# The fold and the spread of the step sums move to another engine, and ScalarE scales the transposed sequence tile by the step sizes

## The reference

```python
scale = max(max|w| / 127, 1e-8)                  # per table row
h  = clip(round(w / scale), -127, 127) * scale   # row of the token
x0 = layernorm(h)                                # (h - mean) / sqrt(var + 1e-5)
z, xBC, dt = split(x0 @ in_proj_w.T)
dt = softplus(dt + dt_bias)                      # the step sizes, 6 heads
x, B, C = split(silu(conv4(xBC)))                # 384, 128, 128 channels
A_cum = cumsum(dt * A)
L  = exp(segsum(dt * A))                         # decays, 128 x 128 per head
y  = ((C B^T) * L) @ (x * dt) + D * x            # "x * dt" is what xd holds
h1 = h + gate * rmsnorm(y * silu(z)) @ out_proj_w.T
...                                              # layernorm, two routers, experts
```

## Time and profile before

| what | value |
|---|---|
| median of 3 runs | 1080.34 us (1077.37 to 1080.86) |
| the profiled execution's own time | 1070.86 us |
| its span | 1069.1 us |
| PE busy over the span | 925.8 us (87%) |
| DVE busy | 692.9 us (65%) |
| ACT busy | 583.3 us (55%) |
| POOL busy | 518.9 us (49%) |

### The profile page before, as it was taken

The page is one execution under the profiler, slowest core; times in us unless marked ns, Lnnn a source line. Parts: engine busy times, 40 slices in busy tenths (PEclk is TensorE's granted clock), DMA queues, the critical chain, the costliest instruction groups (busy, mean ns, idle before and its releaser), DMA issues.

```text
span 1069.1 us, 19874 instructions
## 1 busy us (share of the span) xinstructions
PE 925.8 (87%) x5743; PEld 602.2 (56%) x5744; DVE 692.9 (65%) x2047; ACT 583.3 (55%) x1195; POOL 518.9 (49%) x590
## 2 busy tenths in 40 slices
PE   0778898888988998889889788899988999999985
PEld 0233455455544654555445556677766676777774
DVE  3788999999999999999979515576671221212120
ACT  2767886787768767877775343233232323233330
POOL 6232545356354362561522526433427777775552
PEclk9899999999999999999998789999998999999997
DMA  4920011011101110110000122123431212222220
GB/s 101 320 62 5 16 46 43 5 47 46 46 3 45 45 44 5 46 47 31 3 31 30 49 62 79 49 73 110 147 92 48 69 50 66 56 63 77 66 61 18
DMA packets 50001, 61.54 MB, mean 58 GB/s; under 512 B 22524, under 2 KB 41688, under 8 KB 49412
## 3 DMA queue, kind: packets, MB, share of 16 engines
q0 software_dynamic: 16704, 30.54, 10.0%
q1 hardware_dynamic: 28580, 24.93, 7.7%
q10 hardware_dynamic: 4640, 5.13, 1.6%
HBM read 36.24 MB, written 25.92 MB: 58 GB/s over the span
## 4 chain that ended last, share of the span: by engine, by line
PE 43%; DVE 25%; ACT 14%; issue 9%; POOL 6%; DMA 1%; DVEq 0%; ACTq 0%; POOLq 0%
DVE xbc L1429 9%; PE cx L1213 7%; PE yb L1213 7%; PE mm L1201 6%; PE mm L1197 5%; PE sg L1197 4%; POOL list_c L534 4%; PE mm L1051 4%; PE mm L1055 3%; ACT ht L897 2%; DVE mix L1449 2%; ACT h L688 2%; DVE st L1319 2%; DVE ybuf L1462 2%; ACT xbc L716 1%
## 5 line engine op out<-in xcount | busy, mean ns | idle before, releaser
L1429 DVE SCALAR_TENSOR_TENSOR xbc<-mm,cw,xbc 128x508 f32<-128x508 f32 (+2 forms) x231 | 168.5, 741 | 24.1 <-ACT xbc L716 18.2
L1051 PE MATMUL mm<-xt_a,win_a 128*128 128x512 f32 x248 | 145.1, 669 | 37.7 <-DVE xbc L1429 28.8
L897 ACT ACTIVATE ht<-mm,b1s 128x256 f32<-128x256 f32 x102 | 44.7, 472 | 222.2 <-PE sg L1201 219.7
L509 POOL TENSOR_TENSOR ybuf<-ybuf,zs 128x384 f32<-128x384 f32 x64 | 69.5, 1085 | 105.4 <-DVE ybuf L1462 105.3
L586 POOL DMA_INDIRECT xg<-hr_dram,ids x80 | 80.6, 1008 | 80.7 <-DVE res L1756 44.3
L605 POOL DMA_INDIRECT out_dram<-osb,ids_s x80 | 81.9, 1023 | 64.4 <-DVE osb L1766 38.4
L716 ACT ACTIVATE xbc<-mm,cb,cw 128x512 f32<-128x512 f32 x77 | 56.6, 775 | 95.4 <-PE mm L1055 95.4
L1766 DVE TENSOR_TENSOR osb<-cx,res 128x192 f32<-128x192 f32 x40 | 14.2, 356 | 127.3 <-PE cx L1213 125.7
L1197 PE MATMUL mm<-fx_a,w1a_t 128*128 128x256 f32 x240 | 81.9, 424 | 13.7 <-issue 7.6
L1201 PE MATMUL mm<-fx_b,w1b_t 64*128 64x256 f32 x240 | 85.3, 436 | 0.0
L1201 PE MATMUL sg<-fx_b,w1b_t 64*128 64x256 f32 x240 | 85.3, 436 | 0.0
(11 more groups left out here) (271 smaller groups left out, 2056.8 us busy)
## 6 DMA issues: line engine op xcount, KB each, us to landing
hr_dram<-hr SPq DMA_DIRECT2D x16, 768.0 KB
w2s<-in_w2c_dram SPq DMA_DIRECT2D x4, 576.0 KB, 7.8
w2s_u<-in_w2u_dram ACTq DMA_DIRECT2D x4, 576.0 KB
list_c<-fill SPq DMA_DIRECT2D x2, 1032.0 KB, 12.6
list_u<-fill SPq DMA_DIRECT2D x2, 1032.0 KB, 18.9
w1a<-in_w1c_dram SPq DMA_DIRECT2D x4, 384.0 KB, 6.6
w1a_u<-in_w1u_dram ACTq DMA_DIRECT2D x4, 384.0 KB
xg<-hr_dram,ids POOLq DMA_INDIRECT x80, 3.1
```

The source lines that it names most:

```text
L509: nc.gpsimd.tensor_tensor(ybuf[:, p, :, js], ybuf[:, p, :, js], zs[:, p, :, js], ALU.mult).then_inc(s_y2, 1)
L1051: mmul(tile_bank(g2, m)[:, :], win_a[:, column(m):column(m) + P], xt_a[:, p, :], start=True, stop=False)
L1429: ins = stt(out=dst_[:, :, back:L], in0=src[:, :, 0:L - back], scalar=cw[:, m, TAPS - 1 - back:TAPS - back], in1=dst_[:, :, back:L], op0=A ...
```

## The change

- `xd` (L1445, one VectorE instruction for a sequence) is removed from `weights(j)`. A new ScalarE step `steps_in(j)` makes it with six activations of 64 columns, each with a head's step size as its scale. It waits for the `cbm` of the same j (the counter of the chain "ssd") and stands at four places of ScalarE's order: ahead of `decays(0)`, ahead of `squares`, ahead of `start(4)`, and between `decays(3)` and `silus`. TensorE's `y(j)` now waits for both `xd` and `mix`, and `cbx(j)` for both readers of `cx`.
- `sum_rows` on ScalarE keeps `rows_t` and writes one `rows_u`; the six `rows_s` tiles are made from it by two GpSimd instructions (`spread_rows`), which stand ahead of `norm2`. TensorE's `seg` waits for the first or the second of them.
- In `clip` the four instructions with the quantisation scale become one without it. The scale is folded into the norm: `norm1` on GpSimd multiplies the variance by it twice and the reciprocal root once, and adds the scale where it added 1.
- ScalarE's order at the end of a turn is `sum_rows`, `start(6)`, `start(7)`, `from_tp(g1,1,1)`, and turn t = 1 has an order of its own.
- At the start, ScalarE makes one Exp of a column before it waits for anything, and `norm1(0)` stands ahead of the memset of `fill`.

The diff (left out: the semaphore `s_ru`, the load of `seg_c` and the host's making of it):

```diff
--- before.py
+++ after.py
@@ -73,7 +73,7 @@
 ROWS = 32
 
 
-STEPS = dict(quant=2, clip=3, tap=10, soft=9, ssd=4, h1=2, pick1=1, pick2=8, find=6)
+STEPS = dict(norm=3, quant=2, clip=3, tap=10, soft=9, ssd=4, h1=2, pick1=1, pick2=8, find=6)
 
 
 def wait(eng, sem, value):
@@ -221,7 +221,8 @@
         dts = sb("dts", [P, 2, GS, HEADS], c=a)
         sp1, sp2, sp3 = (sb(n, [P, GS, HEADS], c=a) for n in ("sp1", "sp2", "sp3"))
         drep = sb("drep", [P, P], c=a)
-        seg_c = sb("seg_c", [P, 2, 7], c=a)
+        seg_c = sb("seg_c", [P, 2 * HPB + 4], c=a)
+        rows_u = sb("rows_u", [P, P], c=a)
         ybuf = sb("ybuf", [P, 2, ZT, GL], c=a)
         ysq = sb("ysq", [P, ZT, GL], c=a)
         rs = sb("rs", [P, GS], c=a)
...
@@ -486,17 +488,28 @@
 
             def norm1(g):
 
-                p = g % 2
+                p, norm_link = g % 2, Chain(pool, ch["norm"], g, STEPS["norm"])
                 pool.wait_ge(s_ve, g + 1)
                 nc.gpsimd.tensor_scalar(minus1[:, p, :], mv1[:, :, 0], -1.0, None, ALU.mult)
-                nc.gpsimd.tensor_scalar(var1[:, p, :], mv1[:, :, 1], LNEPS, None, ALU.add).then_inc(s_vr, 1)
+                norm_link(nc.gpsimd.tensor_tensor(var1[:, p, :], mv1[:, :, 1], q1[:, 1, :], ALU.mult))
+                norm_link(nc.gpsimd.tensor_tensor(var1[:, p, :], var1[:, p, :], q1[:, 1, :], ALU.mult))
+                nc.gpsimd.tensor_scalar(var1[:, p, :], var1[:, p, :], LNEPS, None, ALU.add).then_inc(s_vr, 1)
                 pool.wait_ge(s_vr, g + 1)
-                nc.gpsimd.tensor_tensor(rstd1[:, p, :], var1[:, p, :], neghalf[:, :], ALU.pow).then_inc(s_rstd, 1)
+                norm_link(nc.gpsimd.tensor_tensor(more1[:, p, :], var1[:, p, :], neghalf[:, :], ALU.pow))
+                nc.gpsimd.tensor_tensor(rstd1[:, p, :], more1[:, p, :], q1[:, 1, :], ALU.mult).then_inc(s_rstd, 1)
                 pool.wait_ge(s_rstd, g + 1)
-                nc.gpsimd.tensor_scalar(more1[:, p, :], rstd1[:, p, :], 1.0, None, ALU.add)
+                nc.gpsimd.tensor_tensor(more1[:, p, :], rstd1[:, p, :], q1[:, 1, :], ALU.add)
                 nc.gpsimd.tensor_tensor(shift1[:, p, :], minus1[:, p, :], rstd1[:, p, :], ALU.mult).then_inc(s_rs1, 1)
 
             def body(t, g1, g2, g3, g4, g5):
+
+                def spread_rows(q):
+                    if g2 is None:
+                        return
+                    pool.wait_ge(s_ru, g2 + 1)
+                    nc.gpsimd.tensor_tensor(rows_s[:, q, :, :], rows_u[:, :].unsqueeze(1).broadcast_to([P, HPB, P]),
+                                            seg_c[:, q * HPB:(q + 1) * HPB].unsqueeze(2).broadcast_to([P, HPB, P]),
+                                            ALU.mult).then_inc(s_rows, 1)
 
                 def gate_y(j):
                     if g3 is None:
@@ -557,6 +570,8 @@
                 if t + 2 < NG:
                     gather(t + 2)
                 gate_y(2)
+                spread_rows(0)
+                spread_rows(1)
                 norm2()
                 gate_y(3)
                 list_tokens()
@@ -625,9 +640,9 @@
                 gather(g)
             nc.gpsimd.iota(tok[:, :, :], pattern=[[L, SEQS], [0, LINE]], base=0, channel_multiplier=1)
             nc.gpsimd.memset(zrow[:, :], 0.0)
+            norm1(0)
             nc.gpsimd.memset(fill[:, :], DUMMY).then_inc(s_clear, 1)
             pool.wait_ge(s_clear, 1)
-            norm1(0)
             pipeline(body)
 
             rms, norm2, list_tokens = body(NG + 2, *groups(NG + 2))
@@ -679,6 +694,7 @@
         @block.scalar
         def _(act):
             act.wait_ge(s_const, 1)
+            nc.scalar.activation(rows_t[:, 0:1], ones[:, 0:1], ACT.Exp)
 
             def rounded(g):
 
@@ -701,6 +717,18 @@
                         last = nc.scalar.activation(dec[:, j % 2, HPB * n:HPB * (n + 1), :],
                                                     bank_[:, 0:HPB * P].rearrange("p (h s) -> p h s", h=HPB), ACT.Exp)
                     last.then_inc(s_e, 1)
+
+                def steps_in(j):
+
+                    if g3 is None:
+                        return
+                    act.wait_ge(ch["ssd"], STEPS["ssd"] * g3 + j + 1)
+                    act.wait_ge(s_dts, g3 + 1)
+                    wait(act, s_yp, GS * g3 + j - 1)
+                    for h in range(HEADS):
+                        last = nc.scalar.activation(xd[:, j % 2, h * HD:(h + 1) * HD], cx[:, P + h * HD:P + (h + 1) * HD],
+                                                    ACT.Copy, scale=dts[:, g3 % 2, j, h:h + 1])
+                    last.then_inc(s_xd, 1)
 
                 def start(m):
 
@@ -736,11 +764,11 @@
                         return
                     act.wait_ge(s_ct, g2 + 1)
                     sums_ = sg1[:, HPB * P:(HPB + 1) * P]
-                    nc.scalar.activation(rows_t[:, :], sums_, ACT.Identity, bias=seg_c[:, 1, 6:7], scale=seg_c[:, 0, 6:7])
-                    for n in range(2 * HPB):
-                        last = nc.scalar.activation(rows_s[:, n // HPB, n % HPB, :], sums_, ACT.Identity,
-                                                    bias=seg_c[:, 1, n:n + 1], scale=seg_c[:, 0, n:n + 1])
-                    last.then_inc(s_rows, 1)
+                    at = 2 * HPB
+                    nc.scalar.activation(rows_t[:, :], sums_, ACT.Identity, bias=seg_c[:, at + 1:at + 2],
+                                         scale=seg_c[:, at:at + 1])
+                    nc.scalar.activation(rows_u[:, :], sums_, ACT.Identity, bias=seg_c[:, at + 3:at + 4],
+                                         scale=seg_c[:, at + 2:at + 3]).then_inc(s_ru, 1)
 
                 def normed():
 
@@ -829,22 +857,28 @@
                     return normed2, squares, from_tp, copy_side, exp_logits
 
                 if t == LAST_SSD:
+                    steps_in(0)
                     decays(0)
                     decays(1)
+                    steps_in(1)
                     normed2()
                     squares()
+                    decays(2)
+                    steps_in(2)
                     from_tp(g5, 2, 0)
-                    decays(2)
                     from_tp(g5, 2, 1)
                     decays(3)
                     copy_side()
+                    steps_in(3)
                     return
 
+                steps_in(0)
                 decays(0)
                 start(0)
                 start(1)
                 decays(1)
                 normed2()
+                steps_in(1)
                 squares()
 
                 from_tp(g5, 2, 0)
@@ -855,20 +889,33 @@
                 normed()
                 copy_side()
 
+                steps_in(2)
                 start(4)
                 exp_steps()
                 start(5)
                 exp_logits()
-                with_rest()
-                from_tp(g1, 1, 0)
-                decays(3)
-                silus()
-                if t + 1 < NG:
+                if t == 1:
+                    from_tp(g1, 1, 0)
+                    decays(3)
+                    with_rest()
                     rounded(t + 1)
-                from_tp(g1, 1, 1)
-                start(6)
-                start(7)
-                sum_rows()
+                    start(6)
+                    start(7)
+                    sum_rows()
+                    silus()
+                    from_tp(g1, 1, 1)
+                else:
+                    with_rest()
+                    from_tp(g1, 1, 0)
+                    decays(3)
+                    steps_in(3)
+                    silus()
+                    if t + 1 < NG:
+                        rounded(t + 1)
+                    sum_rows()
+                    start(6)
+                    start(7)
+                    from_tp(g1, 1, 1)
 
             rounded(0)
             act.wait_ge(s_wa, n_wa)
@@ -962,7 +1009,7 @@
 
                     if g3 is None:
                         return
-                    pe.wait_ge(s_rows, g3 + 1)
+                    pe.wait_ge(s_rows, 2 * g3 + 1 + j // 2)
                     wait(pe, s_e, GS * g3 + j)
                     for b, bank_ in enumerate((sg0, sg1)):
                         r = (2 * (j % 2) + b) * ROWS
@@ -985,6 +1032,7 @@
                     p, js = g3 % 2, slice(j * L, (j + 1) * L)
                     pe.wait_ge(s_xbc, g3 + 1)
                     wait(pe, s_xd, GS * g3 + j)
+                    wait(pe, ch["ssd"], STEPS["ssd"] * g3 + j)
                     mmul(cx[:, 0:P], xbc[:, p, ZT, js], xbc[:, p, ZT + 1, js], start=True, stop=True)
                     for c in range(ZT):
                         last = nc.tensor.transpose(cx[:, (c + 1) * P:(c + 2) * P], xbc[:, p, c, js], ident[:, :])
@@ -994,6 +1042,7 @@
                     if g3 is None:
                         return
                     pe.wait_ge(s_m, GS * g3 + j + 1)
+                    pe.wait_ge(s_xd, GS * g3 + j + 1)
                     wait(pe, s_yd, GS * g3 + j)
                     for h in range(HEADS):
                         r = (h % 2) * HD
```

(8 more changed lines are left out.)

8 lines of the change are left out of this document (4 added, 4 removed).

## The result

| kernel | median | runs from, to | profiled execution | its span |
|---|---|---|---|---|
| before | 1078.86 us | 1074.23 to 1080.86 | 1070.86 us | 1069.1 us |
| after | 1205.08 us | 1201.55 to 1214.02 | 1201.55 us | 1199.8 us |

The change makes the kernel 12.2% slower: the ratio is 1.1218, with a 95% interval of 1.1179 to 1.1258. The medians alone lie 126.2 us apart (a ratio of 1.117) and the profiled executions 130.7, and the profiled one of before is none of its four runs; so the loss is 126 to 131 us. The forecast had been 1176 us, with a range of 1130 to 1218. Its sign and its four serial places were right, and it is 29 us short, by a term that it had left out.

The account below looks back on a forecast made before the run. VectorE was nearest to a bound, waiting on ScalarE. Thirteen turns at +6.2 us gave 81, then +9, +3, +5 and -2: +96 on 1070.86, 1167, carried to the median as 1176 us, range 1130 to 1218.

Parts of the forecast that it names:

- four serial places: Where `steps_in` waits for `cbm` ahead of work VectorE needs: 3.4, 2.1, 0.5 and 1.8 us more a light turn.
- The six activations: ScalarE's `xd` for one sequence, 0.27 us each: 1.6 us for six, with bounds 1.3 and 2.2.
- A: Ahead of `decays(0)`: activations, table load and Exp follow `cbm(0)`, so `mix(0)` starts at 4.2 us, 3.4 later.
- B: Ahead of `squares`: activations, `squares`, `from_tp` and `start(2)` put `conv(2)` 4.5 us after `cbm(1)`, 2.1 later.
- C: Ahead of `start(4)`: activations and `start(4)` put `conv(4)` 2.7 us after `cbm(2)`, 0.5 later.
- D: Between `decays(3)` and `silus`: load, Silus and `rounded` wait for `cbm(3)`; next `cbm(0)` at 10.8 us, 1.8 later.
- The heavy turns: Stage A turns with `pick` (2 us), hidden under VectorE's wait; logits and places add about 0.5: 42.3 against 37.8 us.
- What costs nothing: GpSimd's two products of 1.07 us and about 1 us in `norm1` are covered in the long turn, not in 34 us.
- The two rules of the Trainium skill: Multiply on VectorE, not ScalarE; table load with drain 2.66 us, making turns 2.8 us longer, about 1218 us, left out.
- Back to the busy sums: Rival, 7%: ScalarE serves VectorE in time, whose 3.1 us a turn come back: 1034 to 1065 us.
- Half the loss: Rival, 9%: first load runs ahead of `steps_in(0)`, turn's end is shortened; some 3 us a turn, 1115 to 1140 us.
- More loss: Rival, 6%: pauses lower TensorE's clock or GpSimd's products hold up `clip`; 2 to 4 us more a turn, 1210 to 1235.

Follow-up runs that it names:

- e10: Changed kernel with constant products nobody reads on TensorE, 18 (8 behind the prefixes) ahead of `project(0)`, 8 ahead of the second `to_tp`: 1213.74 us, ratio 1.0723.
- e1: Changed kernel with `xd` back on VectorE and no `steps_in` on ScalarE, the rest of the change kept: 1132.37 us, ratio 0.9938 to before.
- e4: Changed kernel with the first, second and last `steps_in` placed later, behind the work VectorE needs next: 1164.64 us, ratio 1.0188 to before.
- e3: Kernel before with only the work: six ScalarE activations into a spare tile at each of the four places, without waits: 1160.14 us, ratio 1.0180.
- e2: Kernel before with only the waits: ScalarE waits for `cbm(j)` at the four places and copies one column: 1207.37 us, ratio 1.0594.
- e6: Changed kernel with only the last `steps_in` moved, behind `silus`: 1145.93 us, ratio 1.0654 to before.
- e9: Changed kernel with `xd` on ScalarE only for sequences 1 and 2, on VectorE for 0 and 3: 1065.59 us, ratio 0.9920 to before.
- e7: Changed kernel with only the second `steps_in` moved, behind `from_tp(g5,2,0)`: 1216.84 us, ratio 1.0738 to before.
- e11: Changed kernel with the first and the last `steps_in` moved: 1168.65 us, ratio 1.0313 to before.

## The prediction against the measurement, point by point

**What bounds it.** Right: VectorE stood nearest to a bound, and its order against ScalarE's decided. Its busy sum fell by 34 us, less than the 45 I named, and that had no part in the result.

**The six activations**, the cost from both sides: 1.33 us measured, at the lower bound of 1.3, where I took 1.6. One takes 322 ns by its group but they start 0.20 us apart. I had taken the duration of one (264 ns) as the distance between starts. Four places of 0.27 make this 1.1 us a turn too much.

**The places in a light turn**, from the `cbm` ahead of each:

| step | before | forecast | after |
|---|---|---|---|
| A: `cbm(0)` to `mix(0)` | 0.79 | 4.2 | 3.98 |
| `cbm(0)` to `cbm(1)` | 7.06 | 10.5 | 10.05 |
| B: `cbm(1)` to `conv(2)` | 2.39 | 4.5 | 4.21 |
| `cbm(1)` to `cbm(2)` | 9.20 | 11.3 | 13.03 |
| C: `cbm(2)` to `conv(4)` | 2.22 | 2.7 | 2.37 |
| `cbm(2)` to `cbm(3)` | 8.61 | 9.1 | 8.69 |
| D: `cbm(3)` to `clip` | 5.18 | 7.85 | 7.61 |
| `cbm(3)` to the next `cbm(0)` | 9.01 | 10.8 | 12.04 |
| turn | 33.88 | 41.7 | 43.81 |

Each of the four serial places is there, and each comes 0.2 to 0.3 us earlier than forecast, which is the activations' term. **The step that failed** is what comes behind B and D. Behind B I kept the rest of the interval as it had been; it holds TensorE's work up to the side products, 8.81 us at the lower clock for 5.79 in e10, and VectorE waits 1.91 for them. Behind D I put `project(0)` and `cbx(0)` at the old 1.65 us; from 401.59 to the `cbm` at 404.74 it is now 3.15, 1.5 more. So in this turn the two intervals are 1.7 and 1.2 us over the forecast, 2.9 us together, while the other two are 0.9 under it. I had named this mechanism as a rival, with 6% and 2 to 4 us a turn. It was no rival: the forecast's own places B and D make TensorE pause, so the lower clock came with them, and the term belonged in the sum. e10 is the test of it: with the clock up, the turn is 41.02, and in the light turn B is 365.79 - 354.76 = 11.03 us for 11.3 and D is 10.58 for 10.8.

**The heavy turns** I had at 42.3, 0.6 above the light ones at 41.7. Over t = 3 to 14 of after the light ones have a mean of 42.74 and the heavy ones 45.37, so the heavy turn is where the forecast is further out. (The light turn shown, t = 9, is a long one; it only happens to equal the mean of all.) The difference lies at B, 13.82 for 11.43, where in t = 10 the copy of the side products waits 3.19 us for TensorE. In e10 the same means are 40.43 and 41.88, both under the forecast, so this too goes with the clock for the most part.

**The sum**: thirteen turns +107.6 for +81 (the pair of turns before has a mean of 35.85, not 35.75, and all thirteen have 35.53, against which 42.0 would have given +84); t = 15 +11.5 for +9; t = 16 +7.4 for +3; from t = 17 on +3.6 for +5; the start +0.5 for -2. The error at the start is a small one of its kind: the normalised tile is ready earlier (21.26 for 22.66 us), but turn t = 1 has the Silus last in its new order, and the first `cbm` needs them. In all +130.7 for +96, on the profiled execution's own time 1201.55 for 1167. That 1205 still lies inside the range is partly luck: the room at the top was put there for dearer activations, which turned out cheaper, and the clock's term filled it.

**What costs nothing.** GpSimd's cover held: `norm1` ended 14.0 us into the turn (forecast 15.5), ahead of its reader. My warning that it would not in a turn of 34 us was too dark: with turns of 35.2 us in e1, ScalarE's `xn` waited 1.5 us in all for GpSimd over 440 us, and 4.2 in e4.

**The two rules of the Trainium skill.** "ScalarE: Activation LUTs", "Rules for kernel authors", advises against ScalarE for multiplications. The runs agree in part: one VectorE instruction of 557 ns became 1.33 us on ScalarE, and the work by itself cost 21.4 us (e3). Most of the loss lies where that rule does not look, in the waits. The same page, "What ACT_TABLE_LOAD costs", has about 1.38 us of drain beside the load. The trace of after does not show it either: `xd` ends at 362.59, the load starts at 362.61 and lasts 1.28, the Exp starts at 363.90. The 1218 us that this would have given came near the measured time, but for another reason.

**The rivals.** *Back to the busy sums* fell, with the condition that it had named: ScalarE's waits at A and D are 2.08 and 3.10 us, not under 1. *Half the loss* fell: the load stands behind `steps_in(0)`, at 362.61. *More loss* was right in its mechanism, and the time of 1205 is just under its 1210 to 1235, since the activations were cheaper.

**What is open.** The clock's share of the loss is bounded by e10, not measured: its products are themselves work, and the clock is at 0.97, so I take the 44.8 us they gave back as a lower bound, which is argued. Where the further 42 us lie that appear only when waits and work meet (e2, e3 against after) was not taken apart by place; a part of them is probably the clock (over 60 to 560 us it is 0.85 in after, 0.88 in e2 and 0.93 in e3).

## What to carry to other kernels

When work moves to an engine that is less busy, look first at what it has to wait for and at what stands behind it in that engine's list: here the work alone cost 21 us, the wait alone 69, and both 132, and moving the steps behind what the other engine needs next brought back some 100 of the 126. Count the pause of a third engine too, since its next work comes slowly (2.05 for 1.10 us here). Gains of single places don't add up: A gave 13 us, D 55, both 90, so a place that seems worthless may only be covered by another.

## What the runs showed that was not expected

**The clock after short pauses.** In a turn of 44 us with pauses of 2.00 and 4.88 us the granted clock is 0.74 and 0.75 in the stretches with them, 0.53 and 0.56 in the work right behind them, and 0.99 and 1.00 in the two other stretches. Keeping TensorE busy with work that nobody reads made the kernel 45 us faster.

**Six small activations overlap.** One of 64 columns out of PSUM lasts 322 ns, six take 1.33 us, so the next starts after (1.33 - 0.32) / 5 = 0.20.

**Chips differ by stage.** The kernel before has a median of 1074 to 1079 us on two chips and 1132 to 1139 on others. The difference lies in stage B: from the first `cbm` of t = 17 to the end it is 479 to 489 us in kernels profiled on the former and 534 to 546 on the latter, with a granted clock of 0.97 to 0.99 (before, e6, e9) against 0.91 to 0.93 (e1, e4, e7, e10, e11) over 700 to 1000 us. Turns of stage A seem to fit together across the chips; no kernel has a trace on two of them, but up to the first `cbm` of t = 17 e1 takes 4.4 us less than before does on another chip, and its median is 6.3 less than before's on its own. So a ratio is only taken against runs on the same chip, and across chips only turns are compared.
